# A semaphore of its own for the last gather of each batch, and a shorter wait on GpSimd

## The reference

```python
h = _L0_tok_ref(x, ...)                          # 5-wide convolution, relu, batch norm -> (16, 746, 128)
h = h + _L0_attn_ref(_layernorm(h), ...)         # delta-rule attention
h = h + _L0_ffn_ref(_layernorm(h), ...)          # 16 experts, each chooses its tokens
h = h + _L1_attn_ref(_layernorm(h), ...)         # cross attention to video
h = h + _L1_ffn_ref(_layernorm(h), ...)          # 8 experts, top 2 per token
```

```python
k = Sx // num_experts * CAPACITY                                  # 746 // 16 * 2 = 92
affinity = softmax(einsum('bsd,de->bse', x, gate_weight)).transpose(0, 2, 1)
gating, index = jax.lax.top_k(affinity, k)
x_in = jnp.take_along_axis(x[:, None], index[..., None], axis=2)  # the gather
h = gelu(einsum('bekd,edh->bekh', x_in, w1) + b1)
x_e = einsum('bekh,ehd->bekd', h, w2) + b2
out = zeros.at[batch, index].add(gating[..., None] * x_e)         # back to the tokens
```

## Time and profile before

| | us |
|---|---|
| median of 3 runs | 2277.52 |
| lowest, highest | 2276.15, 2278.78 |
| profiled execution | 2272.64 |
| its span | 2270.8 |
| PE busy | 2000.0 (88%) |
| DVE busy | 1607.0 (71%) |
| ACT busy | 1070.6 (47%) |
| POOL busy | 604.2 (27%) |

### The profile page before, as it was taken

One profiled execution on the slowest core, in us unless ns is written; L12 is line 12 of the kernel. 1 busy time (PEld: TensorE's weight loads), 2 busy tenths in 40 slices (PEclk: granted clock), 3 DMA queues, 4 the chain that ended last, 5 costly groups with the idle time before them and its releaser, 6 DMA issues. The chain is left out here.

```text
span 2270.8 us, 54560 instructions
## 1 busy us (share of the span) xinstructions
PE 2000.0 (88%) x20890; PEld 1776.8 (78%) x20890; DVE 1607.0 (71%) x4095; ACT 1070.6 (47%) x2698; POOL 604.2 (27%) x650
## 2 busy tenths in 40 slices
PE   6589999989646988886999999976999999999998
PEld 5488777778534877885777777766999999999998
DVE  4755555654583855565999999986777777777774
ACT  4433333332344555552677766743444444444443
POOL 0002222220015555520343333343212222221220
PEclk9899999999877999997999999997999999999999
DMA  8100000000211111100000000000000000000000
GB/s 185 44 1 12 11 12 11 12 10 1 73 56 38 44 34 39 41 18 1 3 3 3 3 3 3 3 2 1 8 14 7 7 7 14 7 7 14 7 8 15
DMA packets 80355, 44.50 MB, mean 20 GB/s; under 512 B 45801, under 2 KB 74025, under 8 KB 79753
## 3 DMA queue, kind: packets, MB, share of 16 engines
q1 hardware_dynamic: 74248, 29.53, 5.7%
q0 software_dynamic: 5888, 12.07, 2.0%
HBM read 27.20 MB, written 14.38 MB: 18 GB/s over the span
## 5 line engine op out<-in xcount | busy, mean ns | idle before, releaser
L2127 ACT ACTIVATE w<-banks,b 128x384 f32<-128x384 f32 (+1 forms) x512 | 259.6, 572 | 392.9 <-PE banks L2201 392.9
L2183 PE MATMUL banks<-w,w 128*128 128x128 f32 (+1 forms) x3072 | 364.1, 275 | 0.0
L2183 PEld LDWEIGHTS banks<-w,w 128*128 128x128 f32 (+1 forms) x3072 | 350.4, 189 | 9.1 <-issue 8.7
L1710 PE MATMUL banks<-qT,w 64*64 64x128 f32 (+1 forms) x4608 | 267.9, 269 | 13.2 <-DVE eb L1612 8.7
L1710 PEld LDWEIGHTS banks<-qT,w 64*64 64x64 f32 x4608 | 247.3, 134 | 31.0 <-issue 20.8
L1718 PE MATMUL banks<-eb,w 64*64 64x128 f32 (+1 forms) x4608 | 268.9, 270 | 1.0 <-DVE eb L1612 1.0
L1681 POOL TENSOR_TENSOR t<-eb 128x768 f32<-128x768 f32 x96 | 171.8, 1789 | 289.0 <-ACT eb L1658 286.4
L1718 PEld LDWEIGHTS banks<-eb,w 64*64 64x64 f32 x4608 | 244.1, 133 | 1.7 <-DVE eb L1612 1.5
L2024 DVE SCALAR_TENSOR_TENSOR h<-banks,t_wt,h 128x128 f32 (+3 forms) x672 | 183.6, 342 | 83.2 <-PE banks L2183 79.7
L1237 POOL DMA_INDIRECT xg<-xs,rowu x184 | 178.4, 970 | 131.7 <-DMA xg<-xs,rowu 87.8
L1612 DVE TENSOR_TENSOR eb<-eb,rd 128x1536 f32<-128x1536 f32 x96 | 210.9, 2196 | 2.3 <-ACT rd L1669 2.3
(11 more groups left out here) (305 smaller groups left out, 4241.9 us busy)
## 6 DMA issues: line engine op xcount, KB each, us to landing
out<-h SPq DMA_DIRECT2D x16, 320.0 KB
xs<-r_xl SPq DMA_DIRECT2D x16, 192.0 KB, 2.6
h<-in_xT SPq DMA_DIRECT2D x4, 750.0 KB, 15.7
h<-in_xT SPq DMA_DIRECT2D x4, 749.0 KB, 18.6
xg<-xs,rowu POOLq DMA_INDIRECT x184, 2.5
xs<-r_xl SPq DMA_DIRECT2D x16, 128.0 KB
blocks<-NT SPq DMA_DIRECT2D x24, 48.0 KB, 1.9
D<-blocks SPq DMA_DIRECT2D x24, 48.0 KB, 2.0
```

Of the source, the lines that this page charges most:

```text
L1710: last = nc.tensor.matmul(lbanks(n)[place(n, hd), v, 0:wide(n)], k.Kt[half(hd), v, :], qT[half(hd), n // NC % 2, (n % NC) * P:(n % NC) * P ...
L2127: nc.scalar.activation(gb[u % 2][:, f, s * GW:s * GW + NFREE[s]], k.ps[:, order.bank(n), 0:NFREE[s]], ACT.Relu, bias=k.b1_1[:, 2 * e + f:2 ...
L2183: last = nc.tensor.matmul(k.psf[0:n, o:o + P], gb[u % 2][:, f, c * P:c * P + n], k.w2_1[:, 2 * e + f, :], start=(f == 0), stop=(f == 1))
```

## The change

For each batch a second semaphore, `got_last[g]`, is made. The last gather of the batch adds to it and no longer to `got[g]`. GpSimd's wait behind the batch asks for the other gathers alone (three of four, or two of three). TensorE waits for both semaphores before it transposes the batch. No instruction changes its place, and there are six more semaphores.

```diff
@@ -1066,6 +1066,7 @@
         got = [sem(f"got{g}") for g in range(order.BATCHES)]
+        got_last = [sem(f"got_last{g}") for g in range(order.BATCHES)]
@@ -1237,8 +1238,8 @@
                             nc.gpsimd.indirect_dma_start(
                                 out=xg[:, 4 * g + j, :], out_offset=None, in_=k.xs,
                                 in_offset=bass.IndirectOffsetOnAxis(ap=rowu[:, col:col + 1], axis=0),
-                            ).then_inc(got[g], 16)
-                        pool.wait_ge(got[g], 16 * order.count(g) * (p + 1))
+                            ).then_inc(got_last[g] if j + 1 == order.count(g) else got[g], 16)
+                        pool.wait_ge(got[g], 16 * (order.count(g) - 1) * (p + 1))
@@ -1382,7 +1383,8 @@
                     elif kind == "gathered":
                         n = p * order.BATCHES + x
-                        pe.wait_ge(got[x], 16 * order.count(x) * (p + 1))
+                        pe.wait_ge(got[x], 16 * (order.count(x) - 1) * (p + 1))
+                        pe.wait_ge(got_last[x], 16 * (p + 1))
                         if n:
                             pe.wait_ge(t_moved, n)
```

## The result

The changed kernel took 2346.16 us (median of 4 runs, 2342.04 to 2350.36) against 2276.84 us before (2272.78 to 2278.78): ratio 1.0313, 95% interval 1.0297 to 1.033. It is 69 us slower; 26 us faster was forecast.

The account below looks back on a forecast made before the run. TensorE was taken to bound the gather phase, with 43.4 us of waits for gathers. Gains of 13.6 + 2.5 + 8.7 = 24.8 us plus 1.2 us of clock made 26 us: 2277.5 - 26 = 2251.5 us, range 2243 to 2263 us.

Parts of the forecast that it names:

- the replay: TensorE's 48 transposes of gathered rows, restarted with each landing 1.25 us earlier per preceding batch: 24.8 us gained.
- Slower: Rival: with fewer holes, each gather's issue on GpSimd runs into VectorE; some 11 us lost, 2288 us; chance 0.03.
- Hole: GpSimd's pause before a batch's first gather: about 0.6 us instead of 1.8; a batch then takes 5.35 us, not 6.6.
- The second opinion: Landing estimated at 2.15 us for 64 KB: hole 0.30 us, 1.56 us saved per batch, 27.2 us by the replay.
- near 18 us in all: Sign: TensorE's waits at L1389 on gathers fall to this from 43.4 us, 7.1 of it at the start.
- about 25: Sign: GpSimd's wait for the second half's row table grows to about 25 us from 9.7, as GpSimd arrives early.
- from pair 4 on: Sign: pairs of batches in the gather phase take 36 to 37 us each from pair 4 on.
- The sum: Total gain over the gather phase: 24.8 us from TensorE's waits plus 1.2 us from the clock, 26 us.
- 12.3 - 5.0: TensorE's cumulative gain in the replay: 12.3 us after pair 1, of which 5.0 us was won in pair 0.
- three dips of the clock: TensorE's clock falls behind long waits, at 728, 754 (said to be untouched) and 847 us: 6.8 us of work lost.
- +1.2 us: Gain taken for TensorE's clock, out of a possible -2.5 to +6.8 us.
- What it adds: 48 more TensorE waits taken as 0, bounded at 7.2 us; six semaphore clears hidden behind SyncE's 3.8 us barrier wait.

Follow-up runs that it names:

- sessions of the first kind: Measuring sessions whose traces of kernels other than before lose records of landings; waits "remote" occur only there, and the changed kernel took 1.0313 and 1.0334.
- e17: The changed kernel, unaltered, measured again in a later session beside the kernel before: 2241.68 us against 2268.1, ratio 0.9892.
- session F: The session on chip 13 in which e17 and e18 ran beside the kernel before, which took 2268.1 us there.
- e18: The kernel before without any wait of GpSimd behind a batch, with one wait for all rows at the end: 2238.74 us, ratio 0.9873.
- e10: The changed kernel with two waited memsets behind every gather: 2285.25 us, ratio 1.0058.
- e1: The changed kernel with the full wait for all gathers of a batch back on GpSimd: 2290.37 us, ratio 1.0082.
- e5: The kernel before plus 24 gathers that nothing reads behind the last pair, all on one semaphore: ratio 0.9999.
- e6: The kernel before plus 24 gathers that nothing reads behind the last pair, on two semaphores in turn: ratio 0.9991.
- e7: The kernel before plus 24 gathers that nothing reads behind the last pair, with a wait after every four: ratio 1.0031.
- e8: The kernel before, with GpSimd waiting for the batch before the one just issued and two waited memsets behind each gather: 2283.0 us, ratio 1.0056.
- e13: e5 repeated in another session, the kernel before plus 24 unread gathers behind the last pair: 2273.36 us, ratio 1.0008.
- e14: The kernel before with no wait of GpSimd between batches in the last pair: 2267.71 us, ratio 0.998.
- e15: The kernel before with the 24 unread gathers of e5 put ahead of the last pair: 2302.63 us, ratio 1.0148.
- e16: The changed kernel with four waited memsets behind each batch: 2269.32 us, ratio 0.999.
- e9: The changed kernel, unaltered, run again in a session on chip 4: 2343.28 us, ratio 1.0334.
- e12: The kernel before with the change in the last pair alone: 2293.51 us, ratio 1.0094.
- e2: The kernel before, with GpSimd waiting for the batch before the one just issued: 2342.95 us, ratio 1.0322.

## Why the prediction was wrong, and where it was right

**The step that failed** is the replay: "each keeps its own work since the one before it, and starts at the later of 'own work done' and 'rows landed'". It took for granted that nothing but the rows' landing joins the gathers to the other engines. In sessions of the first kind a dense row of gathers also delays signals between the compute engines, up to 12 us from TensorE to ScalarE, and the changed kernel has 124.3 us of waits "remote" where before has none. Why the signals are late stays open. The trace of before has 2943 of 2944 landings recorded, as in the other kind, so it couldn't show it; which session it was taken in isn't on record. No rival named late signals. Slower had 0.03, on a mechanism (gathers run into VectorE) that isn't it: the median gather is 945 ns, 946 before.

**GpSimd**: right. Hole 0.55 to 0.64 us where 0.6 was said; cycle 5.26 us against 5.35. The second opinion, a hole of 0.30 us from the Trainium skill's estimate on the page "DMA: Bandwidth & Descriptors" (section "Anatomy of one DMA — SWDGE (gpsimd) path"), would have the wait over before the last issue ends. It isn't: the trace's landing of 2.5 us was the better number.

**TensorE**: right where signals are in time. In e17 its waits for gathers are three, 14.4 us (6.87 and 4.10 in pair 0, 3.42 in pair 4), against "near 18 us in all"; GpSimd's wait for the second half's row table is 24.5 us (103.1 less 78.6) against "about 25":

```profile
677.17 1.08 PE L1391 MATMUL banks<-ident,xg 128*128 128x128 f32 x4 [6.87 <-DMA xg<-xs,rowu]
682.35 1.08 PE L1391 MATMUL banks<-ident,xg 128*128 128x128 f32 x4 [4.10 <-DMA xg<-xs,rowu]
```

```profile
PE banks L1391 <- DMA xg<-xs,rowu: 14.4, 3, 6.9
```

```profile
POOL rowf L1221 <- ACT place L1290: 103.1, 2, 78.6
```

Pairs 5 and 6 take 36.2 and 36.4 us between first transposes (867.4, 903.6, 940.0), within the 36 to 37 that was said "from pair 4 on". Pair 4 itself takes 42.4 us (825.0 to 867.4), 6 us more: the wait of 3.42 us for a gather, and 2.8 us more of busy time for the same work (37.3 us against 34.5 in pair 5), at a clock of 0.92 instead of 1.00.

**The sum**: 26 us said, 26.4 us between the medians of session F; that the two agree this closely is partly luck, since the terms don't. Between the two profiled executions, of different sessions, the phase is 34 us shorter (334 against 368); 4.5 us of that is before's profiled execution lying above the median of session F. The replay gives 13.6 us when the fifth pair begins and 24.8 at the end; the trace has 18 us there (first transpose to pair 4's: 166.0 us in the earlier trace rows, 825.0 - 677.2 = 147.8 in e17) and 34. Most of the early excess lies in pair 1, which takes 37.9 us instead of 48.8: 10.9 us gained, where the replay has 12.3 - 5.0 = 7.3. Two of the three dips of the clock, 3.4 us of lost work by the prediction, lay in that pair. So the excess is in part the clock. In e17 the first two of the three dips are gone, also the one from 754 us that was said to be untouched. The third isn't gone; it moved with its work to 828 us, behind the wait of 3.42 us, and costs what it did (12 us at 0.72, an estimated 3.4 us of missing clock). Over the phase the clock is 0.94 instead of 0.92; by these means an estimated 20 us of clock are missing instead of 29. +1.2 us was too little.

```profile
728.00:732.00 4.00, 3.85 (x23) 3.17 (x22) 4.00 (x8) 2.89 (x7) 2.90 (x4) 1.00 0.18 50
754.00:759.00 5.00, 5.00 (x36) 4.63 (x36) 4.97 (x11) 3.01 (x11) 3.88 (x4) 1.00 0.18 52
828.00:840.00 12.00, 10.31 (x52) 9.90 (x53) 4.59 (x12) 4.57 (x14) 8.64 (x10) 0.72 0.17 49
825.00:867.40 42.40, 37.30 (x220) 34.76 (x219) 24.80 (x64) 23.31 (x71) 31.10 (x33) 0.92 0.17 50
867.40:903.60 36.20, 34.48 (x219) 32.24 (x218) 24.44 (x64) 23.16 (x70) 26.35 (x27) 1.00 0.17 50
```

**What it adds**: right. The 48 waits of TensorE cost nothing that shows (e18, which has none of them, is 3 us below e17, less than each spreads), and SyncE's wait at the barrier is 3.1 us, in after and in e17, against 3.8, so the six clears are hidden:

```profile
SPq L281 <- PEq L281: 3.1, 1, 3.1
```

## What to carry to other kernels

A drain of GpSimd between batches of gathers looks like pure loss, and in some sessions it is: without it this kernel gains 1.1 to 1.3%. In others the pause keeps the engines' signals nearly in time, and taking it out costs 3%; of the versions here that ran in such a session, only those with a cycle above 6 us had no long delays (e10 none at all, e1 up to 1.61 us), and they gain nothing, so by these runs, all of them recorded, the kernel before is the safe choice. When a change makes transfers denser, look in its trace for waits that end "remote" and for a source view without its landing row, time it without the profiler too, and measure it in more than one session, with a kernel known to go wrong beside each one that goes right: e5 to e8 and e13 to e16 misled for want of that.

## What the runs showed of the hardware that was not expected

- In sessions of the first kind, semaphore signals between compute engines are late while indirect transfers of 64 KB are issued every 1.25 us (some 50 GB/s and a DMA share of 0.19 in after from 700 to 719 us). The same transfers do no harm in e17 (50 to 53 GB/s, share 0.18). The data is not late: the last packet of a gather ended 2.19 us (median) after its issue in e9 and 2.14 us in e17.
- The delay shows by ScalarE's start over the later of TensorE's end and its own last end: at most 0.04 us in before and in e17, up to 12.0 us in after. The second expert matmul starts up to 15.9 us after the later of its input and TensorE's own end in e9, against 0.8 us in e17; which of its signals was late there isn't told apart. Rows of four dense gathers alone, with drains of 1.8 to 2.3 us, bring delays of up to 1.17 us (e12's first seven pairs) and 1.61 us (e1).
- With a pause of 0.6 us between batches the first wait "remote" comes within 10 us (e12, where small delays came before); from the very first gather it takes 19 to 25 us until ScalarE starts over 0.1 us late (e2, after, e9). The long delays go within 4 us of the last gather (e12).
- The loss of records is wider than the late signals: e10 has 2059 of 2944 landings recorded, and 8368 records of the engines' own signals against 8748 in e8, which raises as many, and not one late signal. Whether both have one cause is open. That signals wait behind the landings' updates fits, and so does that they wait behind the profiler's records; neither was shown.
